# A top-31 sparse attention between two mixture layers: the search for the threshold by pairs of scores

## The reference, cut to what matters

```python
x = x + 0.5 * ffn(layernorm(x)); x = x + attn(layernorm(x)); x = x + 0.5 * ffn(layernorm(x))
# attn, with H = 16 heads of D = 16, L = 512 rows, 16 batches, U = int(5 ln 512) = 31
scores = einsum('bhqd,bhkd->bhqk', Q, K) / sqrt(D)
thresh = top_k(scores, U)[0][..., -1:]
scores = where(scores < thresh, -inf, scores)
context = einsum('bhqk,bhkd->bhqd', softmax(scores), V);  return context @ Wo.T + bo
# ffn: gates rw over 16 experts, q, k, v = sums over experts of rw * (h @ proj),
#      causal attention of width 64, then attn * rw through o_proj
```

## Time and profile before

| | |
|---|---|
| median of 3 runs | 4726.12 us (4723.4 to 4728.99) |
| span of the profiled execution, from its first to its last instruction | 4725.1 us |
| VectorE busy | 4393.5 us, 93% |
| TensorE busy | 4132.2 us, 87% |
| ScalarE busy | 3967.9 us, 84% |
| GpSimd busy | 2995.0 us, 63% |
| DMA | 232.66 MB, mean 49 GB/s |

### The profile page before, as it was taken

The page is one execution under the profiler, slowest core; times in us unless marked ns, Lnnn a source line. Parts: engine busy times, 40 slices in busy tenths (PEclk is TensorE's granted clock), DMA queues, the critical chain, the costliest instruction groups (busy, mean ns, idle before and its releaser), DMA issues. The chain is left out here.

```text
span 4725.1 us, 123794 instructions
## 1 busy us (share of the span) xinstructions
PE 4132.2 (87%) x33100; PEld 3423.4 (72%) x33100; DVE 4393.5 (93%) x10203; ACT 3967.9 (84%) x10181; POOL 2995.0 (63%) x4946
## 2 busy tenths in 40 slices
PE   6778899899999889999998999998899989987777
PEld 5556777777777777777777777777777777765555
DVE  2499999999999999999999999999999999999982
ACT  2488889898898889989888998988899889888772
POOL 1445677677667767766776776677677667654440
PEclk8889999999999999999999999999999999988888
DMA  3111111121111111111111111111111111111011
GB/s 100 45 27 35 49 50 53 50 55 50 52 51 51 53 50 55 50 52 51 51 53 50 55 50 52 51 51 53 50 53 50 54 51 51 51 38 26 22 30 50
DMA packets 244162, 232.66 MB, mean 49 GB/s; under 512 B 27123, under 2 KB 176628, under 8 KB 243316
## 3 DMA queue, kind: packets, MB, share of 16 engines
q1 hardware_dynamic: 243444, 224.49, 16.6%
HBM read 214.98 MB, written 9.44 MB: 47 GB/s over the span
## 5 line engine op out<-in xcount | busy, mean ns | idle before, releaser
L1027 DVE MAX8 M<-W 128x8 f32<-128x512 f32 x2688 | 1735.2, 681 | 57.8 <-DVE W L1029 2.5
L679 PE MATMUL pQ<-wf_sb,HS 128*128 128x192 f32 x8192 | 1545.3, 345 | 81.3 <-POOL HS L419 54.1
L679 PEld LDWEIGHTS pQ<-wf_sb,HS 128*128 128x128 f32 x8192 | 1438.3, 203 | 129.5 <-issue 65.9
L1029 DVE MATCH_REPLACE8 W<-M,W 128x512 f32<-128x512 f32 x1664 | 1115.0, 676 | 0.0
L1072 POOL TENSOR_TENSOR XL<-S,LM 128x512 f32<-128x512 f32 x384 | 445.6, 1160 | 908.4 <-ACT LM L909 895.5
L698 PE MATMUL pST<-ident,S 128*128 128x128 f32 x4096 | 747.9, 283 | 15.4 <-ACT S L897 15.4
L924 ACT ACTIVATE OUT<-S,M 128x512 bf16<-128x512 f32 x1024 | 741.5, 724 | 0.0
L928 ACT ACTIVATE S<-S,M 128x512 f32<-128x512 f32 x1024 | 737.2, 720 | 0.0
L700 PE MATMUL pST<-steep,OUT 128*128 128x128 bf16 x4096 | 731.8, 222 | 0.0
L1029 DVE MATCH_REPLACE8 W<-M,S 128x512 f32<-128x512 f32 x1024 | 684.3, 676 | 0.0
L1027 DVE MAX8 M<-S 128x8 f32<-128x512 f32 x1024 | 651.5, 678 | 20.8 <-ACT S L897 10.7
(11 more groups left out here) (267 smaller groups left out, 6585.2 us busy)
## 6 DMA issues: line engine op xcount, KB each, us to landing
RB<-rows_b SPq DMA_DIRECT2D x384, 256.0 KB, 3.3
RB<-rows_a SPq DMA_DIRECT2D x384, 256.0 KB, 3.3
x_b<-in_x SPq DMA_DIRECT2D x64, 128.0 KB, 2.8
out_y<-y SPq DMA_DIRECT2D x64, 128.0 KB, 1.8
wf_sb<-in_wf SPq DMA_DIRECT2D x4, 768.0 KB, 7.4
rows_b<-rwT_b SPq DMA_DIRECT2D x64, 8.0 KB, 1.3
wof_sb<-in_wof SPq DMA_DIRECT2D x1, 1024.0 KB, 7.1
rows_a<-rwT_a SPq DMA_DIRECT2D x64, 8.0 KB, 1.4
```

The costliest lines, as they stand in the source:

```text
L679: mm = nc.tensor.matmul(pQ[:, 0:QKV], HS[:, k % 2, e, i, :], wf_sb[:, i, at:at + QKV], start=k + e + i == 0, stop=(k, e, i) == (3, 3, 1))
L1027: nc.vector.max(m, src[i]).then_inc(s_tk, 1)
L1029: nc.vector.match_replace(W[:, i, :], m, src[i], -BIG).then_inc(s_tk, 1)
```

## The change

The keys of a head are taken in two halves of 256. `KK` holds the first half of K, the difference first minus second, and the second half; GpSimd makes the difference, twice per batch. The matmul of the scores (same shape as before) now gives d = a - b in columns 0 to 255 and b in 256 to 511, where a and b are the scores of a pair of keys. ScalarE makes three copies of 256 columns of each unit in place of one of 512: b to `S`, relu(d) and relu(-d) to the new ring `HL` of 12 entries. A new step SPLIT (slot 5, every 2) on GpSimd makes with three instructions over 256 columns per unit: max(a, b) = b + relu(d), a = max - relu(-d) into `S`, and min(a, b) = b - relu(-d).

VectorE (TOP, now slot 6) then searches in ten passes: the largest sixteen of the 256 maxima with both groups taken out (MAX8, replace, MAX8, replace), the largest sixteen of the 256 minima (MAX8, replace, MAX8, written into 16 columns between maxima and minima), and three passes (MAX8, replace, MAX8) over the 272 columns that hold the remaining maxima and the sixteen minima. The 31st is the second from last entry of the 32. The light way of three in eight units is gone, with its instructions on ScalarE and GpSimd.

Beside it: reciprocals of the sums of gate and softmax are made by VectorE in all tiles; the two means are no steps any more (ScalarE's square takes the sum as its bias, with a scale of -D); the ramp of the gate's logits (L394) goes, and the sum of masks (L399) moves behind the exponential; the negated maximum comes out of VectorE's reduction, so L426 goes; `mixT` is written in place over `RB2`, so that the load of `RB2` waits for TensorE's last matmul on it (`s_yd`) and not for the multiplication, and stands 3 slots ahead of it (before 7); several tiles of the two jobs are shared between them.

```diff
+HI8, HIR, HI16, HIR2, LO8, LOR, LO16, ALL8, ALLR, ALL16 = range(10)
+STEPS = (HI8, LO8, HIR, LOR, HI16, LO16, HIR2, ALL8, ALLR, ALL16)
+ORDER = [(i, k) for k in STEPS for i in range(2)]
+FOLLOWS = {HIR: (HI8,), HI16: (HIR,), HIR2: (HI16,), LOR: (LO8,), LO16: (LOR,), ALL8: (HIR2, LO16), ALLR: (ALL8,), ALL16: (ALLR,)}
...
-SC, EV, TOP, OUTS, GAP, TR, PTE, PV, CT, CTT, CTX = 2, 3, 4, 10, 11, 16, 17, 18, 19, 20, 21
-LOW, LCOPY, LTOP, LPICK, LTH = 6, 6, 8, 9, 10
+SC, EV, SPLIT, TOP, OUTS, GAP, TR, PTE, PV, CT, CTT, CTX = 2, 3, 5, 6, 10, 11, 16, 17, 18, 19, 20, 21
...
-                        nc.scalar.copy(S[:, (4 * c + h) % RING, :], pST[h][:]).then_inc(s_ev, 1)
+                        nc.scalar.copy(S[:, u % RING, HALVES:T], pST[h][:, HALVES:T])
+                        nc.scalar.activation(entry[:, 0:HALVES], pST[h][:, 0:HALVES], ACT.Relu)
+                        nc.scalar.activation(entry[:, HIL:HIL + HALVES], pST[h][:, 0:HALVES], ACT.Relu, scale=-1.0
+                                             ).then_inc(s_ev, 1)
...
+                if at := soon(w, j, "SPLIT", SPLIT, 2, PAIRS * NB):
+                    n, c = at
+                    for u in (2 * c, 2 * c + 1):
+                        entry = HL[:, place(w, u), :]
+                        pool.wait_ge(s_ev, w.count(SPAN, u + 1))
+                        nc.gpsimd.tensor_tensor(entry[:, 0:HALVES], S[:, u % RING, HALVES:T], entry[:, 0:HALVES], ALU.add
+                                                ).then_inc(s_hi, 1)
+                    for u in (2 * c, 2 * c + 1):
+                        entry = HL[:, place(w, u), :]
+                        pool.wait_ge(s_hi, w.count(SPAN, u + 1))
+                        nc.gpsimd.tensor_tensor(S[:, u % RING, 0:HALVES], entry[:, 0:HALVES], entry[:, HIL:HIL + HALVES],
+                                                ALU.subtract)
+                        nc.gpsimd.tensor_tensor(entry[:, HIL:HIL + HALVES], S[:, u % RING, HALVES:T],
+                                                entry[:, HIL:HIL + HALVES], ALU.subtract).then_inc(s_lo, 1)
...
+                        if k == HI8:
+                            held(dve, s_hi, w.count(SPAN, u + 1))
+                        elif k == LO8:
+                            held(dve, s_lo, w.count(SPAN, u + 1))
...
+                if at := tile(J, "rw", w, j):
+                    t, c = at
+                    dve.wait_ge(q["gate_sum"], t + 1)
+                    nc.vector.reciprocal(J.rgs[:], J.gs[:]).then_inc(q["gate_rec"], 1)
+                if at := tile(J, "sc_rec", w, j):
+                    t, c = at
+                    dve.wait_ge(q["sc_exp"], t + 1)
+                    nc.vector.reciprocal(J.rrs[:], J.rs[:]).then_inc(q["sc_rec"], 1)
...
-                    held(sp, s_mix, earlier(w, j, MIXES.values()))
+                    held(sp, s_yd, earlier(w, j, MIXES.values()))
```

More of the change, by code:

```diff
@@ L22 @@
 TOPK = 31
[L23 to L31, removed]
+HALVES = T // 2
+TAIL = 16
+HIL = HALVES + TAIL
+TH = TAIL + TOPK - TAIL - 1
+RANKS = 32
+HI8, HIR, HI16, HIR2, LO8, LOR, LO16, ALL8, ALLR, ALL16 = range(10)
+STEPS = (HI8, LO8, HIR, LOR, HI16, LO16, HIR2, ALL8, ALLR, ALL16)
+ORDER = [(i, k) for k in STEPS for i in range(2)]
+FOLLOWS = {HIR: (HI8,), HI16: (HIR,), HIR2: (HI16,), LOR: (LO8,), LO16: (LOR,), ALL8: (HIR2, LO16), ALLR: (ALL8,), ALL16: (ALLR,)}
 STEEP = 2.0 ** 80
-LOWER = 2.0 ** 40
-STEEPER = 2.0 ** 110
 MASKED = -1.0e30
@@ L144, in earlier, with passed, place @@
     return w.count(k_all, c_all)
[L147 to L159, removed]
+def passed(w, u, k):
+    return w.count(SPAN // 2 * len(ORDER), u // 2 * len(ORDER) + ORDER.index((u % 2, k)) + 1)
+def place(w, u):
+    return (SPAN * w.lo + u) % RINGH
 def fill(n, w, j):
@@ L205, in build @@
         S = sb("S", P, RING, T)
-        W = sb("W", P, 2, T)
-        M8 = sb("M8", P, RING, 8 * ROUNDS)
+        HL = sb("HL", P, RINGH, HIL + HALVES)
+        M8 = sb("M8", P, RING, RANKS)
         OUT = sb("OUT", P, HALF, T, dtype=BF16)
[L209 to L218, removed]
         PTs = sb("PTs", P, HG, T)
@@ L402, in layer @@
                 eng.wait_ge(q["gate_exp"], t + 1)
-                ns.tensor_tensor(J.em[:], J.eg[:], J.mk[:], ALU.mult).then_inc(q["gate_em"], 1)
+                ns.tensor_tensor(J.ep[:], J.eg[:], J.pos[:], ALU.mult).then_inc(q["gate_em"], 1)
+                wait(eng, q["gate"], 5 * t + 5)
+                eng.wait_ge(q["gate_em"], 2 * t + 1)
+                ns.tensor_tensor(J.em[:], J.ep[:], J.fb2[:], ALU.add).then_inc(q["gate_em"], 1)
             if at := mine("rw"):
                 t, c = at
-                held(eng, q["gate_sum"], t + 1)
-                inverse(ends, J.rgs, J.gs).then_inc(q["gate_rec"], 1)
                 held(eng, q["gate_rec"], t + 1)
@@ L822, in leave @@
                     act.wait_ge(q["full"], n)
-                    nc.scalar.copy(J.rwT[:], F[0:E, 0:P]).then_inc(q["read"], 1)
+                    nc.scalar.copy(J.rwT, F[0:E, 0:P]).then_inc(q["read"], 1)
                 if at := tile(J, "qkT", w, j):
@@ L833, in leave @@
                     act.wait_ge(q["full"], n)
-                    nc.scalar.copy(J.Sr[:, 0:wide], F[:, 0:wide]).then_inc(q["read"], 1)
+                    nc.scalar.copy(Sr[:, 0:wide], F[:, 0:wide]).then_inc(q["read"], 1)
                 if at := tile(J, "pT", w, j):
@@ L838, in leave @@
                     act.wait_ge(q["full"], n)
[L839 removed]
+                    nc.scalar.copy(PTf[:, 0:wide], F[:, 0:wide]).then_inc(q["read"], 1)
                 if at := tile(J, "attT", w, j):
@@ L843, in leave @@
                     act.wait_ge(q["full"], n)
-                    nc.scalar.copy(J.attT[:], F[:, 0:P]).then_inc(q["read"], 1)
+                    nc.scalar.copy(attT[:], F[:, 0:P]).then_inc(q["read"], 1)
                 if at := tile(J, "y", w, j):
@@ L1046, in _ @@
             nc.gpsimd.memset(ones[:], 1.0)
-            for k in range(8):
-                nc.gpsimd.memset(iota[:, k:k + 1], float(k - TH - 1))
-            nc.gpsimd.memset(lower[:], LOWER)
             nc.gpsimd.memset(minus_half[:], -0.5)
-            nc.gpsimd.memset(minus_one[:], -1.0)
             nc.gpsimd.memset(steep[:], 0.0).then_inc(s_cst, 1)
@@ L1066, in slot @@
             def slot(w, j):
[L1067 to L1085 removed]
+                for c in range(2):
+                    if at := at_proj(f"K{c}", w, j):
+                        pool.wait_ge(jobs["b"].sem["read"], fill("b", w, j) + 1)
+                        nc.gpsimd.tensor_tensor(KK[:, c, 1, :], KK[:, c, 0, :], KK[:, c, 2, :], ALU.subtract
+                                                ).then_inc(s_kd, 1)
```

268 lines of the change are left out of this document (106 added, 162 removed).

## The result

The changed kernel takes 5193.82 us (median of 4 runs, 5192.09 to 5197.63) against 4725.61 us before (median of 4 runs, 4723.40 to 4728.99): a ratio of 1.0992, 95% interval 1.0977 to 1.1008. The forecast was 4348 us, range 4190 to 4520. The profiled execution has a span of 5190.6 us.

The account below looks back on a forecast made before the run. VectorE bounds the kernel at 275.2 us per batch; after the change GpSimd, at 248, would in full batches. 322 us outside the search + 2.93 x 241 + 13.07 x 254 = 4348 us, range 4190 to 4520.

Parts of the forecast that it names:

- VectorE's sum: VectorE's search: ten passes cost 3.59 us per unit, 239 to 241 us per batch with the rest, down from 275.
- Rival D: VectorE's half passes lose 0.1 us each to latency: period 304 us, 5186 us; chance 0.07 together with Rival C.
- GpSimd's split: GpSimd's three new instructions per unit, 192 per batch at 0.58 us: 111 us, with 97 and 132 as ends.
- the 132 of the forecast: GpSimd's work per full batch once 62 us of removed instructions are taken from 193.8 us.
- my other bound: GpSimd's split instruction by the line through 1024 and 512 columns: 554 ns, a distance of 0.505 us.
- small edits: Dropped means, VectorE's reciprocals and the later load of `RB2`: each taken as worth nothing in the sum.
- The K differences are two more, nothing: GpSimd's two differences of the halves of K per batch were taken to add nothing to its work.
- The sum of the middle: In 13.07 fully loaded batches the period falls from 275.2 to 254 us: GpSimd's 248 and something for keeping step.
- 2 to 3%: Allowance in the middle for three nearly equally full engines (248, 240, 239 us) that keep step by semaphores.
- The ends: In the other 2.93 batches, outside the full load, VectorE sets a period of 241 us.
- Rival C: GpSimd's new instructions delay TensorE, which falls to 1.2 GHz: period 284 to 290 us, 4740 to 4818; 0.07 with Rival D.
- thirteen more slow groups: TensorE's extra matmul groups per batch, 1.77 us more each, needed to grow its 261 us by 23.

Follow-up runs that it names:

- e6: e5 with each of GpSimd's three split instructions made one over both units of a pair, in place of two of 256 columns; 4699 us.
- e2: The changed kernel with VectorE's reciprocals ahead of the search in each slot, not behind it; 4932 us.
- e1: The changed kernel with the reciprocals of the gate and softmax sums back on GpSimd; 5074 us.
- e8: The kernel before with only the reciprocals moved to VectorE, behind the search in the slot; 4830 us.
- e3: The changed kernel with GpSimd's K difference made two slots later than ScalarE's copy of K; 5031 us.
- e5: The changed kernel with both moves: VectorE's reciprocals ahead of the search and the K difference two slots later; 4786 us.
- e15: e6 with GpSimd's output product ahead of the split, and without the restore of the scores' first half (output not the reference's); 4362 us.
- e7: e5 without GpSimd's instruction that restores the first half of the scores (output not the reference's); 4529 us.
- e13: The changed kernel with one move alone: GpSimd makes the output product ahead of the split of the pair; 5045 us.
- e10: e6 with VectorE, not GpSimd, restoring the first half of the scores in every second pair; 4804 us.
- e12: e10 with GpSimd's output product also made ahead of the split in its slot; 4542 us.

## Why the prediction was wrong, by its steps

**VectorE's sum was right.** Ten passes were to cost 3.59 us per unit and a batch 239 to 241 us; VectorE's work measured 243, and the passes are 409 to 430 ns long as from the slope of the earlier trace rows. No latency shows between dependent passes. Rival D gave 5186 us, near the measured time, but by the wrong mechanism: the 284 + 536 us in which VectorE stands idle end with the split's outputs, none of it with a pass of its own.

**GpSimd's split was mis-sized.** I took 0.58 us of distance, the row of the same shape, over the line through 16 and 1024 columns, which gave 0.69. It is 0.69 (length 733 to 736 ns). 192 x 0.11 = 21 us per batch; the work measured 266 us instead of 248 less the 5 of gaps, in all 23 too low. What was to go from GpSimd did go: 266 less 133 for the splits is about the 132 of the forecast. The row that I trusted, 627 ns, has an operand that is broadcast along its innermost axis; the new instructions have not. I had seen this difference and not priced it; that it is the reason was not tried by itself. e6 confirms the line: 1281 ns at 512 columns, with 221 and 2372 ns at its ends. The row of 512 columns with 1160 ns, my other bound, has one operand of 2 bytes, likewise not tried by itself. Alone it is 23 x 13.07 = 301 of the 846 us by which the forecast was short.

**The step that failed is the one on small edits: "two waits now stand in VectorE's queue (reciprocals) ... ScalarE's sums are one slot ahead, 4 us, so nothing".** I asked who has to wait for the reciprocal's inputs, and not how long the reciprocal itself would stand behind what its engine already had in that slot, and who waits for its result in the same slot. GpSimd does, with the next split behind it. In 2400 us of the middle it waits 131.6 us there, 17.0 us per batch of 310.5. A place ahead of the search alone (e2) is worth 261 us, undoing the move to VectorE (e1) 120; and the same move costs 107 us in the kernel before, which has no splits (e8). Only job b stops: its `rw` falls in the even slots, where the search is, and job a's in the odd ones.

**A second wait I priced at nothing in passing.** "The K differences are two more, nothing" counted their work, 0.73 us each, and not that they wait in the slot in which their source is made: 222 us in 32 places, 14.5 us per batch in the middle (e3, 162 us). Both waits together give back 407 of the 468 us lost (e5).

**The sum of the middle.** Work 266, rw_b 17.0, KK 14.5, ScalarE's logits 3.4, its own results 4, gaps about 5: 310. Against the forecast of 254, made of 243 of work and 11 of gaps and idle time, that is 23 more work and 33 more waits, 301 and 431 us in 13.07 batches. Such a sum closes for every engine, so it does not say by itself which one sets the pace: TensorE's 310 are 260 of work and 46 of waits for GpSimd's results. What speaks for the two waits are e1, e2, e3 and e5. My allowance of "2 to 3%" for engines that keep step was the fourth error: e15, with the known waits gone and no engine overloaded, still has 4% above the fullest engine's 243 us, and e7, without the product's move and the wide split, 7%.

**The ends.** I had 2.93 batches at VectorE's 241 us. The search now runs from 179.5 to 5066.9 us. Its first batch and its last two, each from the first pass over the maxima on:

```profile
179.53:491.03 311.50, 219.73 (x1595) 170.94 (x1594) 238.96 (x933) 211.78 (x573) 225.39 (x331) 0.83 0.10 27
4519.60:4804.70 285.10, 234.39 (x1888) 184.98 (x1886) 237.65 (x934) 217.35 (x584) 234.51 (x316) 0.91 0.14 38
4804.70:5066.92 262.22, 201.26 (x1622) 153.10 (x1622) 233.90 (x923) 195.12 (x512) 198.61 (x273) 0.84 0.10 28
```

The last two are shorter than the middle, as forecast, but not 241, and VectorE is 83% and 89% busy. The first is as long as the middle's although GpSimd has only 225 us of work in it: there it stops for `rgs_b` for 39 us in five places. So GpSimd's work alone doesn't make the period. What else holds at the ends was not tried.

**Rival C was the right family.** It said that the new instructions stand in GpSimd's queue ahead of what TensorE waits for. TensorE's wait for `rw_b`, which I had expected to shrink with the light way, grew from 129 to 259 us in the whole kernel and that for the product from 19 to 242, and its clock fell from 0.96 to 0.93, not under 0.9. I gave it, with D, 0.07, with the argument that splits and `HS` fall in different slots. The product falls in the splits' slots; moving it ahead gave 149 us (e13). But its price, thirteen more slow groups or 23 us of TensorE's busy time per batch, did not come: TensorE is busy for 260.4 us where it was 251.7. What it lost were waits. How the loss divides between TensorE's waits and those in GpSimd's own queue stays open: e2 and e3 shorten both, e8 costs 107 us with slack on GpSimd, and e13 gains 149 us with GpSimd's work unchanged.

## What to carry to other kernels

A moved instruction has three prices: its duration, what waits behind it on its new engine, and how long it stands itself behind that engine's long work while another in-order queue stops for its result. The last is the distance from one engine's slot to the other's, and instructions of 0.14 us, sixteen per batch, can cost 261 of 5194 us by their place alone: put short ones that release another engine ahead of the long ones. For a price at a new size take the line through like rows (same types, no broadcast along the innermost axis), not the single row with the right shape. And before moving elementwise work to VectorE look for two-input instructions on GpSimd beside it.

## What the runs showed of the hardware that was not expected

- GpSimd's f32 two-input instruction costs about 0.19 us and 2.13 ns per column: 221 ns at 16, 733 at 256, 1281 at 512, 2372 at 1024. Two pieces of 256 columns in one instruction cost 1281 ns, not 2 x 733.
- The one 256-column instruction of GpSimd with an operand broadcast along the innermost axis took 627 ns, the others 732 to 736; no run changes the broadcast alone.
- VectorE's two-input instruction over 2 x 256 columns and GpSimd's two-input ones did not run side by side: 670 ns with none under way, median 1624 and up to 2750 ns in all (e10); of those that began inside an `HS` in e12, each ended 0.54 to 0.56 us behind it.
- VectorE's MAX8 and MATCH_REPLACE8 in place, over 256 and 272 columns, hold the line of 16 and 512 columns (160 and 680 ns): 409 to 430 ns.
